# One stage of an eight-stage kernel rewritten: sparse attention with its loop unrolled and its work spread over three engines

## The chip, the core and the metric

The kernel runs on one core of a Trainium2 chip. Its engines are TensorE (PE; PEld is its weight load), VectorE (DVE), ScalarE (ACT), GpSimd (POOL) and SyncE (SP, which issues DMAs). They run at the same time and wait for one another on semaphores. PE writes to PSUM (eight banks, ps in the names), which DVE and ACT read and POOL does not. The metric is the time of one execution in microseconds (us); 0.2% of it is 8 us.

## The reference

Eight stages work one after another on X, 2048 tokens by 128 channels: delta, ternary, chunks, ternary, sparse, local, global, local. The change is in the fifth, sparse attention, x = x + attn(layernorm(x)), with one batch of 2048 tokens and H = 16 heads of DK = 8 channels. Cut to what is computed:

```python
Q, K, V = (proj(Wq, bq), proj(Wk, bk), proj(Wv, bv))
l2 = jnp.linalg.norm(Q, axis=-1)
prob = jnp.exp(jax.nn.log_softmax(Q, axis=-1))
entropy = -jnp.sum(prob * jnp.log(prob + 1e-09), axis=-1)
var = jnp.var(Q, axis=-1, ddof=1)
q_scores = 0.5 * l2 + 0.3 * entropy + 0.2 * var
factor = jnp.clip(jnp.round(q_std / (q_mean + 1e-06) * 10), 3, 10)
_, top_idx = jax.lax.top_k(q_scores, 10)
scores = jnp.einsum('bhud,bhld->bhul', Q_sparse, K) / np.sqrt(DK)
out = jnp.einsum('bhud,bhld->bhud', softmax(scores), V)
return scatter(out at top_idx, rank < factor) @ Wo.T + bo
```

q_std and q_mean are of q_scores over the tokens; Q_sparse is Q at the ten chosen tokens of each head; the second einsum weighs V.

## The kernel before

All stages are built one after another by build_program from the list ORDER; each is a function that opens blocks. In a block each engine has its own straight list of instructions, kept in the order written; no scheduler moves them. Between blocks all engines meet, and clear_signals (L45) zeroes the semaphores. X stays in SBUF as 16 tiles of 128 tokens.

sparse_attention (L1742) has three parts. A short block transposes the four weight matrices (L1793, L1799) and POOL fills the row of token numbers tokrow (L1785). A hardware loop of four passes (L1803) follows, each over a group of four tiles. In a pass DVE copies the group (L1838) and normalises it (normalize_tiles, L1169, with inv_sqrt, L84: ten small ops). PE transposes it, ACT evicts it to xnT (L1827), PE makes q and v (L1814, L1815) and k (L1818), DVE adds the biases (L1843, L1844) and makes the three scores of each head from q: the norm of q by its squares and one more inv_sqrt, the variance, and the entropy, for which ACT does Exp (L1831) and Ln (L1833). PE transposes the scores (L1821), DVE keeps them in qs (L1877). Only one buffer and one bank of each kind exist, and link makes DVE wait for its own last instruction.

The third part is the selection block, from L1902 on. DVE finds the ten largest scores of each head by two rounds of eight (L1974 to L1978), then mean and variance of the scores (L1981 to L1984) and u, the number of ranks kept (L1985 to L1995). With the indices spread over all partitions (L1997, L1910, L2000) it builds sel, a one-hot of 16 tiles by 160 columns (L2002), by which PE gathers the chosen queries (L1921). The 160 queries are handled as two halves of 80 (g = 0, 1): scores against all keys (L1929), row maximum (L2017), Exp on ACT (L1964), scaling (L2022), transposes (L1936) and three copies (L2025). Both halves use banks 0 to 3 for scores and 4 to 6 for transposes, so half 1 waits for half 0. Then the contexts in one sum of 160 columns (L1941), the output matrix (L1946), and the scatter by the one-hot selT (L2010) into four banks (L1954), which DVE adds to X (L2033) after the bias (L2031).

## Time and profile before

| | |
|---|---|
| median of 3 runs | 3910.77 us (3905.14 to 3911.5) |
| profiled execution | 3910.19 us |
| its span, first to last instruction | 3908.4 us |
| mean granted clock of TensorE | 0.943 |
| busy in the span | PE 3422.6 (88%), DVE 2563.9 (66%), ACT 1828.0 (47%), POOL 1582.6 (40%) |
| sparse stage | from about 1300 to 1501 us of the span |

The profiled execution's time stands 1.8 us above its span, which leaves out what lies before the first and after the last instruction. A busy share is an average over all eight stages; for the change, the rows of the stage alone count.

### The profile page before, as it was taken

How to read it: one execution, taken by the hardware profiler on the slowest of the kernel's cores; microseconds unless marked ns; L12 is line 12 of the kernel's file. 1: busy time of each engine (PE TensorE's matmuls, PEld its weight loads, DVE VectorE, ACT ScalarE, POOL GpSimd, SP SyncE). 2: the span in 40 equal slices, each digit the busy share in tenths (PEclk: the TensorE clock that was granted, in tenths of full speed). 3: DMA queues.
4: the chain of work that ended last, by engine and by line, in shares of the span. 5: the costliest groups of instructions: out<-in, count | busy, mean ns of one | idle time of the engine just before them, and what ended most of it. 6: DMA issues, size and time to landing. Idle time of an engine off the chain costs nothing. (4 is left out here: it accounts for less than half of the span.)

```text
span 3908.4 us, 61702 instructions
## 1 busy us (share of the span) xinstructions
PE 3422.6 (88%) x23454; PEld 2133.2 (55%) x23454; DVE 2563.9 (66%) x4849; ACT 1828.0 (47%) x3254; POOL 1582.6 (40%) x1085
## 2 busy tenths in 40 slices
...
GB/s 93 1 1 1 1 1 1 1 1 1 1 51 3 5 0 44 2 2 2 38 1 1 1 1 1 1 1 1 1 1 1 1 1 1 1 44 2 2 2 12
DMA packets 21485, 31.44 MB, mean 8 GB/s; under 512 B 8418, under 2 KB 17932, under 8 KB 19724
## 3 DMA queue, kind: packets, MB, share of 16 engines
...
## 5 line engine op out<-in xcount | busy, mean ns | idle before, releaser
L2924 POOL TENSOR_TENSOR global_acc_pool<-global_acc_pool,global_probs 128x1024 f32<-128x1024 f32 x320 | 776.2, 2426 | 470.7 <-ACT global_probs L2877 453.9
L2877 ACT ACTIVATE global_probs<-global_ps 128x1024 f32<-128x1024 f32 x512 | 524.4, 1024 | 883.3 <-PE global_ps L2750 822.2
L2972 DVE TENSOR_REDUCE global_part<-global_ps 128x2 f32<-128x1024 f32 x512 | 624.5, 1220 | 429.7 <-PE global_ps L2732 429.6
L2750 PE MATMUL global_ps<-global_q,global_k 64*128 64x512 f32 x2048 | 522.4, 588 | 0.0
L2761 PE MATMUL global_ps<-global_probs,global_v 128*64 128x512 f32 x2048 | 495.7, 605 | 0.0
L2732 PE MATMUL global_ps<-global_khh,global_qhh 64*128 64x512 f32 x1024 | 324.9, 631 | 35.7 <-DVE global_part L2972 33.6
L994 DVE COPY_PREDICATED delta_Y<-delta_tri,delta_ps 128x512 f32<-128x512 uint32 x192 | 140.3, 731 | 290.9 <-PE delta_ps L533 290.9
L2748 PE MATMUL global_ps<-global_mrow,global_first 64*128 64x512 f32 x1024 | 323.6, 629 | 0.0
L900 POOL TENSOR_TENSOR delta_gm<-C_tile,delta_g 128x1024 f32<-128x1024 f32 x16 | 30.3, 1896 | 719.2 <-PE delta_ps L453 685.5
L2761 PEld LDWEIGHTS global_ps<-global_probs,global_v 128*64 128x64 f32 x2048 | 124.2, 136 | 282.6 <-issue 161.5
L2732 PEld LDWEIGHTS global_ps<-global_khh,global_qhh 64*128 64x128 f32 x1024 | 97.9, 188 | 322.7 <-DVE global_part L2972 259.1
L811 ACT ACTIVATE delta_T<-delta_ps 128x512 f32<-128x512 f32 x192 | 114.7, 597 | 270.2 <-PE delta_ps L496 270.2
L2750 PEld LDWEIGHTS global_ps<-global_q,global_k 64*128 64x128 f32 x2048 | 193.9, 186 | 86.0 <-issue 61.3
L375 PE MATMUL delta_ps<-delta_wconv,delta_x1T 128*128 128x512 f32 x512 | 232.7, 599 | 6.3 <-PEq L50 5.1
L2301 ACT ACTIVATE local_sm<-local_ps,local_nb,local_rn 128x128 f32<-128x128 f32 x512 | 226.3, 463 | 15.9 <-DVE local_nb L2487 14.5
L2924 DVE TENSOR_TENSOR global_acc<-global_acc,global_probs 128x1024 f32<-128x1024 f32 x128 | 194.8, 1522 | 10.1 <-ACT global_probs L2877 10.1
L518 PE MATMUL delta_ps<-delta_T,delta_NT 128*128 128x128 f32 x1536 | 195.1, 278 | 0.7 <-ACT delta_T L811 0.7
L533 PE MATMUL delta_ps<-delta_Y,delta_NTp 128*128 128x128 f32 x1536 | 192.8, 279 | 0.0
L2748 PEld LDWEIGHTS global_ps<-global_mrow,global_first 64*128 64x128 f32 x1024 | 96.4, 185 | 163.4 <-issue 151.9
L518 PEld LDWEIGHTS delta_ps<-delta_T,delta_NT 128*128 128x128 f32 x1536 | 183.1, 191 | 4.2 <-ACT delta_T L811 0.9
L533 PEld LDWEIGHTS delta_ps<-delta_Y,delta_NTp 128*128 128x128 f32 x1536 | 181.4, 191 | 0.0
L375 PEld LDWEIGHTS delta_ps<-delta_wconv,delta_x1T 128*128 128x128 f32 x512 | 94.5, 192 | 102.8 <-issue 100.7
...
## 6 DMA issues: line engine op xcount, KB each, us to landing
delta_cw<-in_conv_taps SPq DMA_DIRECT2D x4, 1024.0 KB, 10.5
...
global_cos<-in_rope_cos SPq DMA_DIRECT2D x2, 512.0 KB, 10.5
...
```

The lines of the kernel that those rows point to most:

```text
L375: mm = pe.matmul(banks(bank), x1T[:, P * n + j:P * n + j + P], wconv[:, j, column:column + 512], start=(j == 0), stop=(j == TAPS - 1))
L518: mm = pe.matmul(bank_heads(NTP_BANK[s], 1)[:, h % 4, :], NT[:, h, :], T[:, h, :], start=True, stop=True)
L533: mm = pe.matmul(bank_heads(DELTA_BANK[s], 1)[:, h % 4, :], NTp[:, h, :], Y[:, n % 2, h, :], start=True, stop=True)
L994: dve.copy_predicated(Y[:, n % 2, half(s), :], over_middle(tri[:, l + 1, :], 4), bank_heads(DELTA_BANK[s], 1)).then_inc(PAIRED["Y_ready"][ ...
L2301: ins = act.activation(sm[:, k % 2, g, :], ps[:, SC + part, P * i:P * i + P], ACT.Exp, bias=nb[:, k % 2, g:g + 1], scale=rn[:, k % RN, hea ...
L2732: mm = pe.matmul(ps[:, 5 + s, :], qhh[own, u % 2, P * qt:P * qt + P], khh[own, group_of(u) % 2, BLK * c:BLK * c + BLK], start=True, stop=True)
L2748: pe.matmul(ps[:, 2 * (at % 2) + s, :], first[own, :], mrow[own, u % 2, :], start=True, stop=False)
L2750: mm = pe.matmul(ps[:, 2 * (at % 2) + s, :], k2[own, group_of(u) % 2, P * k:P * k + P], q[own, u % 3, :], start=False, stop=True)
L2761: mm = pe.matmul(ps[own, 4, :], v[:, k, HD * g:HD * g + HD], probs[:, at % RING, BLK * s:BLK * s + BLK], start=(k == 0), stop=(k == TILES ...
L2877: act.activation(probs[:, at % RING, :], ps[:, 2 * (at % 2):2 * (at % 2) + 2, :].rearrange("p b n -> p (b n)"), ACT.Exp).then_inc(S["probs ...
L2924: ins = eng.tensor_tensor(sums[:, u % 2, :], sums[:, u % 2, :], probs[:, at % RING, :], ALU.add)
L2972: dve.tensor_reduce(part[:, u % 2, r % SLOTS, :], ps[:, 5:7, :], X_AXIS, ALU.max)\
```

## The change

The loop and the short block before it become one block over all 16 tiles. The normalisation is done once for 16 tiles, with inverse_root (nine ops), as the ternary stage does it. Each kind of PSUM result has two banks in turn. The biases of q and v become matmuls with one row (ones by the bias) into the same bank. ACT evicts q, its square, v and k. POOL adds the output bias to X, subtracts the mean, squares the difference, and multiplies probabilities by their logarithms. One inverse_root over 256 columns serves the norms of all groups. In the selection block ACT makes sum and squared spread of the scores, sel is made in quarters, POOL makes selT, each half has four banks of its own, the contexts are two sums of 80 columns, and X is added by group. The rank numbers are loaded in the first block.

```diff
--- before
+++ after
+GROUPS = TILES // GROUP
+TURN_BANKS, Q_BANKS, V_BANKS, K_BANKS = (0, 1), (2, 3), (4, 5), (6, 7)
+GATHER_BANK, IDX_BANK, COLS_BANK = 4, 5, 6
...
-with nc.Fori(0, TILES // GROUP) as t:
...
+        pool.memset(tiny[:], 1e-9).then_inc(S["constants"], 1)
+        pool.iota(tokrow[:], [[1, TOKENS]], base=0, channel_multiplier=0,
+                  allow_small_or_imprecise_dtypes=True)
+        pool.wait_ge(E["arena_loaded"], C["arena_count"])
+        pool.wait_ge(S["xn_ready"], GROUPS)
+        pool.tensor_tensor(X[:], X[:], over_middle(bo, TILES), ALU.add).then_inc(S["bias_added"], 1)
+        for g in range(GROUPS):
+            pool.wait_ge(S["mean_ready"], g + 1)
+            q8 = q_all[:, GROUP * g:GROUP * g + GROUP, :].rearrange("p t (h e) -> p (t h) e", e=HD)
+            pool.tensor_tensor(dev[:, g], q8, over_inner(s1[:, g], HD), ALU.subtract)\
+                .then_inc(S["centred"], 1)
+            pool.wait_ge(S["centred"], 2 * g + 1)
+            pool.tensor_tensor(dev[:, g], dev[:, g], dev[:, g], ALU.mult).then_inc(S["centred"], 1)
+        for g in range(GROUPS):
+            pool.wait_ge(S["log_ready"], g + 1)
+            pool.tensor_tensor(lp[:, g], lp[:, g], e8[:, g], ALU.mult).then_inc(S["weighed"], 1)
...
+        def project(g, banks, i, bias):
+            for t in range(GROUP):
+                own = ps[:, banks[g % 2], P * t:P * t + P]
+                pe.matmul(own, xnT[:, g % 2, P * t:P * t + P], wT[:, i, :], start=True, stop=False)
+                mm = pe.matmul(own, ones[0:1, :], bias[0:1, :], start=False, stop=True)
+            return mm
+        def project_all(g):
+            pe.wait_ge(S["xnT_ready"], g + 1)
+            if g >= 2:
+                pe.wait_ge(S["q_ready"], g - 1)
+            project(g, Q_BANKS, 0, bq).then_inc(S["q_ps"], 1)
+            if g >= 2:
+                pe.wait_ge(S["v_ready"], g - 1)
+            project(g, V_BANKS, 2, bv).then_inc(S["v_ps"], 1)
+            if g >= 2:
+                pe.wait_ge(S["k_ready"], g - 1)
+            pe.matmul(ps[:, K_BANKS[g % 2], :], wT[:, 1, :], xnT[:, g % 2, :], start=True, stop=True)\
+                .then_inc(S["k_ps"], 1)
...
+        for g in range(GROUPS):
+            turn_rows(g)
+            if g == 0:
+                pe.wait_ge(S["wT_ready"], 1)
+            project_all(g)
...
+        def keep_rows(g):
+            act.wait_ge(S["xnT_ps"], g + 1)
+            if g >= 2:
+                act.wait_ge(S["k_ps"], g - 1)
+            act.activation(xnT[:, g % 2, :], ps[:, TURN_BANKS[g % 2], :], ACT.Copy).then_inc(S["xnT_ready"], 1)
+        def keep_projections(g):
+            tiles = slice(GROUP * g, GROUP * g + GROUP)
+            act.wait_ge(S["q_ps"], g + 1)
+            act.activation(q_all[:, tiles, :].rearrange("p t d -> p (t d)"), ps[:, Q_BANKS[g % 2], :], ACT.Copy)
+            act.activation(sq[:, g].rearrange("p h e -> p (h e)"), ps[:, Q_BANKS[g % 2], :], ACT.Square)\
+                .then_inc(S["q_ready"], 1)
+            act.wait_ge(S["v_ps"], g + 1)
+            act.activation(v_all[:, tiles, :].rearrange("p t d -> p (t d)"), ps[:, V_BANKS[g % 2], :], ACT.Copy)\
+                .then_inc(S["v_ready"], 1)
+            act.wait_ge(S["k_ps"], g + 1)
+            act.activation(kT_all[:, GT * g:GT * g + GT], ps[:, K_BANKS[g % 2], :], ACT.Identity, bias=bk)\
+                .then_inc(S["k_ready"], 1)
+        for g in range(GROUPS):
+            keep_rows(g)
+            keep_projections(g)
+        for g in range(GROUPS):
+            act.wait_ge(S["shifted"], g + 1)
+            act.activation(e8[:, g], e8[:, g], ACT.Exp).then_inc(S["exp_ready"], 1)
+        act.wait_ge(S["constants"], 1)
+        for g in range(GROUPS):
+            act.wait_ge(S["prob_ready"], g + 1)
+            act.activation(lp[:, g], e8[:, g], ACT.Ln, bias=tiny[:]).then_inc(S["log_ready"], 1)
+        for g in range(GROUPS):
+            act.wait_ge(S["scoreT_ps"], g + 1)
+            act.activation(qs[:, GT * g:GT * g + GT], ps[0:H, g, :], ACT.Copy).then_inc(S["scoreT_ready"], 1)
...
+        def sums(g):
+            dve.wait_ge(S["q_ready"], g + 1)
+            q8 = q_all[:, GROUP * g:GROUP * g + GROUP, :].rearrange("p t (h e) -> p (t h) e", e=HD)
+            link(dve.tensor_reduce(s1[:, g], q8, X_AXIS, ALU.add))
+            dve.tensor_scalar(s1[:, g], s1[:, g], 1.0 / HD, None, ALU.mult).then_inc(S["mean_ready"], 1)
+            link(dve.tensor_reduce(m8[:, g], q8, X_AXIS, ALU.max))
+            dve.tensor_tensor(e8[:, g], q8, over_inner(m8[:, g], HD), ALU.subtract).then_inc(S["shifted"], 1)
+            dve.tensor_reduce(s2[:, g], sq[:, g], X_AXIS, ALU.add)
+        def probs(g):
+            dve.wait_ge(S["exp_ready"], g + 1)
+            link(dve.tensor_reduce(den8[:, g], e8[:, g], X_AXIS, ALU.add))
+            link(dve.reciprocal(den8[:, g], den8[:, g]))
+            dve.tensor_tensor(e8[:, g], e8[:, g], over_inner(den8[:, g], HD), ALU.mult)\
+                .then_inc(S["prob_ready"], 1)
+        def variances(g):
+            dve.wait_ge(S["centred"], 2 * g + 2)
+            return dve.tensor_reduce(var8[:, g], dev[:, g], X_AXIS, ALU.add)
+        def entropies(g):
+            dve.wait_ge(S["weighed"], g + 1)
+            return dve.tensor_reduce(ent[:, g], lp[:, g], X_AXIS, ALU.add)
+        for g in range(GROUPS):
+            sums(g)
+            if g:
+                probs(g - 1)
+        probs(GROUPS - 1)
+        every = {n: a[:].rearrange("p g h -> p (g h)") for n, a in
+                 (("s2", s2), ("l2", l2), ("var8", var8), ("ent", ent))}
+        link(dve.tensor_scalar(every["s2"], every["s2"], SMALLEST, None, ALU.max))
+        link(inverse_root(dve, link, every["s2"], every["l2"], t1[:], t2[:]))
+        link(dve.tensor_tensor(every["l2"], every["l2"], every["s2"], ALU.mult))
+        for g in range(GROUPS):
+            ins = variances(g)
+        link(ins)
+        link(dve.tensor_scalar(every["var8"], every["var8"], 0.2 / (HD - 1), None, ALU.mult))
+        link(dve.scalar_tensor_tensor(out=every["l2"], in0=every["l2"], scalar=0.5, in1=every["var8"],
                                       op0=ALU.mult, op1=ALU.add))
...
+        for g in range(GROUPS):
+            ins = entropies(g)
+        link(ins)
+        dve.scalar_tensor_tensor(out=score[:].rearrange("p t h -> p (t h)"), in0=every["ent"], scalar=-0.3,
+                                 in1=every["l2"], op0=ALU.mult, op1=ALU.add).then_inc(S["score_ready"], 1)
...
+    for part in range(4):
+        pe.wait_ge(A["sel_ready"], part + 1)
+        for t in range(4 * part, 4 * part + 4):
+            mm = pe.matmul(ps[:, GATHER_BANK, 0:H * TOP], q_all[:, t, :], sel[:, t, :],
+                           start=(t == 0), stop=(t == TILES - 1))
+    mm.then_inc(A["gather_ps"], 1)
+    pe.wait_ge(A["u_ready"], 1)
...
+    def turn_probs(g):
         pe.wait_ge(A["probs_ready"], g + 1)
...
+        for t in range(TILES):
+            mm = pe.transpose(ps[:, 4 * g + t // 6, HALF * (t % 6):HALF * (t % 6) + HALF],
+                              probs[:, g, P * t:P * t + P], ident[0:HALF, 0:HALF])
         mm.then_inc(A["probsT_ps"], 1)
...
+    def contexts(g):
+        pe.wait_ge(A["probsT_ready"], g + 1)
+        for t in range(TILES):
+            mm = pe.matmul(ps[:, 4 * g + 3, 0:HALF], v_all[:, t, :], probsT[:, g, t, :],
+                           start=(t == 0), stop=(t == TILES - 1))
+        mm.then_inc(A["o_ps"], 1)
+    def rows_out(g):
+        pe.wait_ge(A["oT_ready"], g + 1)
+        pe.matmul(ps[0:HALF, 5 + g, 0:DIM], oT[:, 8 * g:8 * g + 8, :].rearrange("p h r -> p (h r)"),
+                  wT[:, 3, :], start=True, stop=True).then_inc(A["ow_ps"], 1)
+    turn_probs(0)
+    contexts(0)
+    turn_probs(1)
+    contexts(1)
+    rows_out(0)
+    rows_out(1)
...
+    act.activation(spare[:], qs[:], ACT.Copy, accum_out=total[:]).then_inc(A["total_ready"], 1)
+    act.wait_ge(A["total_ready"], 1)
+    act.activation(nst[:], total[:], ACT.Copy, scale=-1.0 / TOKENS).then_inc(A["nmean_ready"], 1)
+    act.wait_ge(A["nmean_ready"], 1)
+    act.activation(spare[:], qs[:], ACT.Square, bias=nst[:], accum_out=ur[:]).then_inc(A["spread_ready"], 1)
...
+@block.gpsimd
+def _(pool):
+    for g in range(2):
+        pool.wait_ge(A["cols_ready"], 1)
+        pool.tensor_scalar(selT[:, g, :], tokrow[:], idxcol[:, g:g + 1], None, ALU.is_equal)\
+            .then_inc(A["selT_ready"], 1)
...
+    dve.tensor_tensor(zexp[:], over_middle(topf[:, 0:TOP], H), over_inner(ident[0:H, 0:H], TOP), ALU.mult)\
+        .then_inc(A["z_ready"], 1)
+    dve.wait_ge(A["idx_ps"], 1)
+    dve.tensor_copy(idx[:], ps[:, IDX_BANK, 0:H * TOP]).then_inc(A["idx_ready"], 1)
+    dve.wait_ge(A["idx_ready"], 1)
+    for part in range(4):
+        own = slice(4 * part, 4 * part + 4)
+        dve.tensor_tensor(sel[:, own], over_middle(idx[:], 4), over_inner(tokid[:, own], H * TOP), ALU.is_equal)\
+            .then_inc(A["sel_ready"], 1)
...
+    def scale_probs(g):
         dve.wait_ge(A["probs_exp"], g + 1)
...
+        own = srow[:, g:g + 1]
+        link(dve.reciprocal(own, own))
+        link(dve.tensor_tensor(own, own, valid[:], ALU.mult))
+        dve.tensor_scalar(probs[:, g, :], probs[:, g, :], own, None, ALU.mult).then_inc(A["probs_ready"], 1)
+    def keep_probs(g):
         dve.wait_ge(A["probsT_ps"], g + 1)
         for b, n in enumerate((6, 6, 4)):
...
+            ins = dve.tensor_copy(probsT[:, g, 6 * b:6 * b + n, :],
+                                  ps[:, 4 * g + b, 0:HALF * n].rearrange("p (i r) -> p i r", r=HALF))
         ins.then_inc(A["probsT_ready"], 1)
...
+    scale_probs(0)
+    scale_probs(1)
+    keep_probs(0)
+    keep_probs(1)
+    own_heads(0)
+    own_heads(1)
+    dve.wait_ge(S["bias_added"], 1)
+    for g in range(GROUPS):
+        dve.wait_ge(A["y_ps"], g + 1)
+        own = X[:, GROUP * g:GROUP * g + GROUP, :].rearrange("p t d -> p (t d)")
+        dve.tensor_tensor(own, ps[:, g, :], own, ALU.add)
```

**ACT, groups.** Before, one pass of the loop (run four times):

```order
L1827 ACT_TABLE_LOAD
L1827 ACTIVATE sparse_xnT<-sparse_ps 128x512
L1829 ISA
L1829 ACTIVATE sparse_kT_all<-sparse_ps,inputs_arena 128x512
L1831 ACTIVATE sparse_e<-sparse_e 128x512
L1833 ACT_TABLE_LOAD
L1833 ACTIVATE sparse_lp<-sparse_e,sparse_tiny 128x512
```

Now, from the last group's evictions (the first of five rows, like those of the three groups before) to the end of the block:

```order
L1867 ACTIVATE sparse_xnT<-sparse_ps 128x512
L1872 ACTIVATE sparse_q_all<-sparse_ps 128x512
L1873 ACTIVATE sparse_sq<-sparse_ps 128x512
L1876 ACTIVATE sparse_v_all<-sparse_ps 128x512
L1879 ACTIVATE sparse_kT_all<-sparse_ps,inputs_arena 128x512
L1887 ACTIVATE sparse_e<-sparse_e 128x512 x4
L1891 ACT_TABLE_LOAD
L1891 ACTIVATE sparse_lp<-sparse_e,sparse_tiny 128x512 x4
L1894 ACTIVATE sparse_qs<-sparse_ps 16x512 x4
```

All four Exps (sparse_e) stand behind the evictions of all four groups.

**PE, selection block.** Before:

```order
L1910 MATMUL sparse_ps<-sparse_zexp,C_tile 128x160
L1914 MATMUL sparse_ps<-C_tile,sparse_idx 80x1 x2
L1916 MATMUL sparse_ps<-sparse_u,C_tile 80x1
L1921 MATMUL sparse_ps<-sparse_sel,sparse_q_all 128x160 x16
L1929 MATMUL sparse_ps<-sparse_kT_all,sparse_qexp 80x512 x4
L1936 MATMUL sparse_ps<-C_tile,sparse_probs 128x80 x16
L1929 MATMUL sparse_ps<-sparse_kT_all,sparse_qexp 80x512 x4
L1936 MATMUL sparse_ps<-C_tile,sparse_probs 128x80 x16
L1941 MATMUL sparse_ps<-sparse_probsT,sparse_v_all 128x160 x16
```

Now, from the same place:

```order
L1983 MATMUL sparse_ps<-sparse_zexp,C_tile 128x160
L1988 MATMUL sparse_ps<-sparse_sel,sparse_q_all 128x160 x16
L1993 MATMUL sparse_ps<-C_tile,sparse_idx 80x1 x2
L1995 MATMUL sparse_ps<-sparse_u,C_tile 80x1
L2001 MATMUL sparse_ps<-sparse_kT_all,sparse_qexp 80x512 x8
L2008 MATMUL sparse_ps<-C_tile,sparse_probs 128x80 x16
L2015 MATMUL sparse_ps<-sparse_probsT,sparse_v_all 128x80 x16
L2008 MATMUL sparse_ps<-C_tile,sparse_probs 128x80 x16
L2015 MATMUL sparse_ps<-sparse_probsT,sparse_v_all 128x80 x16
```

The scores of both halves run together, the column matmuls stand behind the gather, and each half has its own context sum.

## Rows read from the trace of the kernel before

**Rows 1.** Windows of the stage: busy us of each engine (records), granted clock, DMA.
```profile
1300.21:1304.39 4.18, 0.63 (x4) 0.42 (x4) 0.01 (x2) 0.78 (x2) 1.87 (x2) 0.78 0.02 6
1304.39:1422.91 118.52, 28.84 (x104) 19.78 (x104) 76.24 (x228) 20.69 (x25) 0.00 (x0) 0.56 0.00 0
1422.91:1500.88 77.97, 35.49 (x188) 28.14 (x188) 43.30 (x62) 5.70 (x6) 0.00 (x0) 0.70 0.00 0
```
**Rows 2.** Timeline, start of the second pass: start, us, line, output<-input [idle before].
```profile
1334.25 0.43 DVE L1838 COPY sparse_xg<-X 128x512 f32 x1 [1.59 <-PEq L50]
```
**Rows 3.** Timeline of the ternary stage just before.
```profile
1283.33 3.19 DVE L1271 BATCH_NORM_STATS2 ternary_gstats<-X 128x6 f32<-128x128 f32 x16 [1.93 <-PEq L50]
...
1289.85 7.08 DVE L1287 TENSOR_SCALAR ternary_xn<-X,ternary_gmv,ternary_grstd 128x128 f32<-128x128 f32 x16
...
1291.11 1.26 POOL L1261 TENSOR_TENSOR X<-X,inputs_tern_bias 128x512 f32<-128x512 f32 x1 [36.48 <-DVE ternary_xn L1287]
```
**Rows 4.** Timeline of the first pass, xn to projections.
```profile
1308.37 1.11 DVE L1180 TENSOR_SCALAR sparse_xn<-sparse_xg,sparse_gmv,sparse_grstd 128x128 f32<-128x128 f32 x4
...
1311.34 0.79 PE L1814 MATMUL sparse_ps<-sparse_wT,sparse_xnT 128*128 128x128 f32 x2 [0.69 <-ACT sparse_xnT L1827]
...
1314.91 1.68 PE L1818 MATMUL sparse_ps<-sparse_xnT,sparse_wT 128*128 128x512 f32 x2
```
**Rows 5.** Windows, columns as in rows 1: clock before and after its changes.
```profile
1306.00:1316.00 10.00, 5.78 (x22) 4.63 (x22) 3.77 (x20) 0.60 (x1) 0.00 (x0) 0.50 0.00 0
1316.00:1319.00 3.00, 0.59 (x1) 0.00 (x0) 2.93 (x6) 1.32 (x2) 0.00 (x0) 0.96 0.00 0
...
1459.60:1463.00 3.40, 0.00 (x0) 0.00 (x0) 2.44 (x2) 0.88 (x1) 0.00 (x0) 1.00 0.00 0
1463.00:1466.00 3.00, 0.07 (x1) 0.07 (x2) 1.59 (x3) 1.18 (x2) 0.00 (x0) 0.50 0.00 0
```
**Rows 6.** Groups by line, DVE in the loop: busy us, mean ns, idle before.
```profile
L1859 DVE TENSOR_TENSOR sparse_t<-sparse_qg,sparse_s 128x512 f32<-128x512 f32 x4 | 2.8, 693 | 0.1
...
L1852 DVE TENSOR_REDUCE sparse_s<-sparse_t 128x64 f32<-128x512 f32 x4 | 2.7, 686 | 0.1
...
L1864 DVE RECIPROCAL sparse_s<-sparse_s 128x64 f32<-128x64 f32 x4 | 2.2, 553 | 0.1
...
L95 DVE SCALAR_TENSOR_TENSOR sparse_r<-sparse_r,sparse_s 128x64 f32<-128x64 f32 x4 | 0.9, 226 | 0.1
```
**Rows 7.** Groups by line, ACT in the loop.
```profile
L1827 ACT ACT_TABLE_LOAD x4 | 5.1, 1283 | 18.2 <-PEq L50 18.2
...
L1829 ACT ACTIVATE sparse_kT_all<-sparse_ps,inputs_arena 128x512 f32 x4 | 2.7, 687 | 21.0 <-PE sparse_ps L1818 21.0
...
L1827 ACT ACTIVATE sparse_xnT<-sparse_ps 128x512 f32<-128x512 f32 x4 | 2.4, 597 | 20.7 <-PE sparse_ps L1810 20.7
```
**Rows 8.** Timeline of the selection part.
```profile
1434.89 2.27 DVE L1981 TENSOR_REDUCE sparse_st<-sparse_qs 16x1 f32<-16x2048 f32 x1
...
1444.58 0.31 DVE L1997 TENSOR_TENSOR sparse_zexp<-sparse_topf,C_tile 16x160 f32<-16x160 f32 x1
...
1446.24 2.83 DVE L2002 TENSOR_TENSOR sparse_sel<-sparse_idx,inputs_arena 128x2560 f32<-128x2560 f32 x1
...
1449.12 6.38 PE L1921 MATMUL sparse_ps<-sparse_sel,sparse_q_all 128*128 128x160 f32 x32 [1.91 <-DVE sparse_sel L2002]
...
1472.61 2.29 DVE L2017 TENSOR_REDUCE sparse_mrow<-sparse_ps 80x1 f32<-80x2048 f32 x1 [2.62 <-PE sparse_ps L1929]
...
1475.12 1.96 ACT L1964 ACTIVATE sparse_probs<-sparse_ps,sparse_mrow 80x2048 f32<-80x2048 f32 x1 [10.94 <-DVE sparse_mrow L2018]
...
1478.92 2.39 PE L1936 MATMUL sparse_ps<-C_tile,sparse_probs 80*128 80x80 f32 x16 [6.35 <-DVE sparse_probs L2022]
...
1483.03 6.49 PE L1941 MATMUL sparse_ps<-sparse_probsT,sparse_v_all 128*128 128x160 f32 x32 [1.71 <-DVE sparse_probsT L2025]
...
1491.07 7.41 PE L1954 MATMUL sparse_ps<-sparse_ow,sparse_selT 80*128 80x128 f32 x64 [0.47 <-ACT sparse_ow L1967]
```

More of the change, by code:

```diff
@@ new lines, in _ @@
+                    link(ins)
+                    link(dve.tensor_scalar(B["var"][:], B["mv"][:, :, 1], LN_EPS, None, ALU.add))
+                    link(inverse_root(dve, link, B["var"][:], B["rstd"][:], B["tmp"][:, 0, :], B["tmp"][:, 1, :]))
+                    for t in range(TILES):
+                        ins = dve.tensor_scalar(xn[:, t, :], X[:, t, :], B["mv"][:, t, 0:1], B["rstd"][:, t:t + 1],
+                                                ALU.subtract, ALU.mult)
+                        if t % GROUP == GROUP - 1:
+                            ins.then_inc(S["xn_ready"], 1)
@@ L1917, in _ @@
                     .then_inc(A["cols_ps"], 1)
-                pe.wait_ge(A["sel_ready"], 1)
-                for i in range(TILES):
-                    mm = pe.matmul(ps[:, 7, 0:H * TOP], q_all[:, i, :], sel[:, i, :],
-                                   start=(i == 0), stop=(i == TILES - 1))
-                mm.then_inc(A["q_ps"], 1)
                 pe.wait_ge(A["qexp_ready"], 1)
+                pe.wait_ge(A["cols_ready"], 1)
                 for g in range(2):
-                    if g:
-                        pe.wait_ge(A["probs_exp"], 1)
@@ L1953, in _ @@
+                turn_probs(0)
[4 more added lines that the diff above has]
+                rows_out(1)
+                pe.wait_ge(A["ow_ready"], 2)
+                pe.wait_ge(A["selT_ready"], 2)
+                for t in range(TILES):
                     for g in range(2):
-                        mm = pe.matmul(ps[:, i // 4, P * (i % 4):P * (i % 4) + DIM], selT[:, g, P * i:P * i + P],
-                                       ow[:, g, :], start=(g == 0), stop=(g == 1))
@@ new lines, in _ @@
+                for g in range(2):
+                    act.wait_ge(A["ow_ps"], g + 1)
+                    act.activation(ow[:, g, :], ps[0:HALF, 5 + g, 0:DIM], ACT.Copy).then_inc(A["ow_ready"], 1)
+            @block.gpsimd
+            def _(pool):
+                for g in range(2):
+                    pool.wait_ge(A["cols_ready"], 1)
+                    pool.tensor_scalar(selT[:, g, :], tokrow[:], idxcol[:, g:g + 1], None, ALU.is_equal)\
+                        .then_inc(A["selT_ready"], 1)
```

265 lines of the change are left out of this document (87 added, 178 removed).

## The prediction

> **What bounds the kernel now.** First the windows of the stage [rows 1]. The sparse stage stands alone: VectorE (DVE) leaves the ternary stage at 1300.21, four loop passes run from 1304.39 to 1422.91, the selection part ends at 1500.88. Nothing of another stage overlaps it, so what it saves comes off the span one for one. In the 118.5 us of loop DVE is busy 76.2, TensorE (PE) 28.8, ScalarE (ACT) 20.7, GpSimd (POOL) 0: one chain runs DVE, PE, ACT, DVE in turn, 29.6 us a pass. Then the timeline: 1.6 us between passes go to clearing semaphores and the branch [rows 2]. The selection part is the same kind of chain, 78.0 us with DVE busy 43.3.
>
> **The change, first part.** The loop becomes one block. I follow its longest chain.
>
> 1. DVE starts about 1.2 us after 1300.21 (a block change costs 1.6 with a branch [rows 2]): 1301.4. Statistics and root chain for 16 tiles took 6.5 us in the ternary stage (1283.33 to 1289.85 [rows 3]), now once and not four times a shorter one: 1307.9. Four tiles of xn, four transposes and one eviction: from 1308.37 to 1311.34 before, 3.0 [rows 4]. Projections start at 1310.9.
> 2. Projections. q and v bias move from DVE to 1-row matmuls, so PE has 32 records a group where it had 16. A record took 0.22 us before (16 from 1311.34 to 1314.91 [rows 4]); the clock was at 0.50 of full speed, 1.2 GHz, and rose to 2.4 GHz 4.8 us after the projections began, too late for them [rows 4, 5]. Now there is work left then: 4.8 us hold 21.5 records, the other 10.5 go at the fast rate of 0.116 (64 records in 7.41 [rows 8]), 1.2 us, and k at 0.86 (half of its 1.7): group 0 ends at 1317.8. The next group can't start at once: ACT evicts k (0.69) before it evicts the next transposes (0.60) [rows 7]. A cycle is 32 x 0.116 + 0.86 + 0.69 + 0.60 + 0.2 of handing over = 6.1 us with PE idle 1.4 of it; between 1459.60 and 1463.00 an idle PE still had 1.00 [rows 5], so I take the clock as kept. Three cycles: 1336.1.
> 3. All Exps stand on ACT behind all evictions, as the order shows. So DVE does the sums of groups 0 and 1, then waits about 12 us for the first Exp: k's eviction and Exp, 0.7 each, give 1337.5. This is what is late next.
> 4. DVE then has, of what the loop did, two groups of sums (three reduces, one subtract at 0.69, one small op at 0.2, gaps: 3.1 each) and four of normalising (reduce 0.69, reciprocal 0.55, product 0.69, gaps: 2.05) [rows 6]: 14.4 us, 1351.9. The variance's subtract and square and the product with the logarithm are POOL's now, q's square ACT's, the copies of X and q are gone.
> 5. One root chain on 128x256, not four on 128x64. No such row exists; between 0.226 (64 wide) and 0.693 (512 wide) [rows 6] lies 0.43 for the eight two-input ops, and I take 0.3 for the three others: 4.6 with gaps. The bounds are 2.5 (all as 64 wide) and 7.9 (all as 512 wide). Then eight reduces of 0.69 and three small ops: 6.9. 1363.4.
> 6. POOL at work beside DVE. While POOL added the bias in the ternary stage, 16 tiles of xn took 7.08 us against 1.11 for four alone (4.4 for 16), a factor 1.6 [rows 3, 4]. On the path some 8 us of DVE's work fall beside POOL's: from nothing, if its products don't mind, to 5 us at that factor; no row decides, I take the middle, 2.5. 1365.9. POOL's X add, and its work on groups 0 and 1, lie beside DVE's wait and cost nothing; without that wait (an earlier Exp) they would meet the DVE sums.
> 7. Sixteen score transposes at 0.22 and ACT's last copy, 4.4; block change 1.2: the selection part starts at 1371.5 instead of 1422.91. **51 us saved.**
>
> The Trainium skill, in SBUF — State Buffer, section Who interferes with whom, holds that a DVE instruction in a two-port mode or with two SBUF inputs shares a port with POOL and that one of them blocks; in GPSIMD Engine Reference, section When to use GPSIMD, it advises elementwise work on DVE. By that rule step 6 would be a rival rather than 2.5 us; it is the second below.
>
> **The change, second part**, in us after its start. The count's mean and variance leave DVE's path: 1434.89 to 1444.58, 9.7 us, now two ACT passes beside the top-k search, the short rest behind sel. sel comes in quarters: PE starts three quarters of 2.83 earlier, 2.1. So the gather starts at 26.2 - 9.7 - 2.1 = 14.4 and, at 6.4 as before, ends at 20.8 [rows 8]. The u chain (18 ops of 1 column, about 0.18) ends at 19.9 under it. Column matmuls, copies and the valid mask follow: scores start at 22.0. Each half is four matmuls of 512 columns, 0.86 each at the fast rate as k above: half 0 is ready 3.7 later. Maximum and Exp from 25.7: 2.5 and 2.1, to 30.3 (before, 1472.61, 1475.12 and the Exp's end with its sum [rows 8]). Half 1's scores now use other banks, 29.2; its maximum ends at 31.7, Exp at 33.9. DVE scales half 0 only after that maximum, 1.7: 33.4; transposes 2.4, 35.9; copies 1.7, 37.6 (1478.92 to 1483.03 for the two [rows 8]). The contexts are two sums of 32 records of 80 columns. No such record exists; 0.20 at the low clock (160 columns: 6.49 for 32 in all), 0.12 at the high as above: bounds 3.7 and 6.5, I take 5.4 for the first, since PE is cold from its wait [rows 5], 4.5 for the second. First: 43.0. Transposes of half 1, hot, 1.3; copies 1.6: 46.0; second context 50.5. oT, output product, copy 1.1; scattering 7.4, then the last quarter's add 0.8 [rows 8]: 59.8 against 78.0. selT runs on POOL from 22.0: by POOL's 1.3 us for 512 elements of a sum [rows 3] at most 10 us for both, done well before 51. **18 us saved.** The cleared semaphores and the rank load lie beside other work. The bias to X, 2.3 us, was hidden before.
>
> **Sum.** 51.4 + 18.2 = 69.6. The profiled execution took 3910.2, of which the span is 3908.4 and 1.8 lies around it; the median of the runs is 3910.8, so it stands for them. 3910.2 - 69.6 gives 3841.
>
> **Rivals.**
> - **PE stays at 1.2 GHz in the projections** (0.14). For it: every cycle has an idle stretch, and the loop's projections never left 0.50 before their end [rows 4, 5]. Against it: the clock outlived an idle stretch of 3.4 us. A cycle becomes 32 x 0.223 + 1.7 + 1.5 = 10.3, three times 4.2 more, and 2 in group 0: 3856. TensorE: Matmul & The Clock Gate, section A second HAM failure mode, of the Trainium skill tells of just this, a matmul stream throttled again by short idles between bank changes.
> - **POOL and DVE take turns** (0.12). POOL's products for groups 2 and 3 and the four with the logarithm come while DVE is on the path: eight of 1.3 us [rows 3], 10.4, and selT against the scaling of half 0, 3. In place of 2.5 that gives 3852.
> - **Less in the way than taken** (0.12). No contention (2.5), contexts at 3.7 each (2.5), the root chain at its lower bound (2): 3834.
> - **Slower** (0.03). Four passes of one loop body become straight code. If an engine had to wait for its code, each wait on the path as long as ACT's 4.6 at the head of a pass (18.2 for four [rows 7]), the gain of 69.6 would be gone from the sixteenth wait on; twenty make 92 us, 3933. Against it: the selection part is straight code already, and its 64 scatter records ran with no gap [rows 8].
> - That the change doesn't do what it says: three engines get work but in part take turns, DVE waits 12 us for ACT. That is in the forecast.
>
> **How the numbers follow.** The forecast holds 0.59, its own range 3833 to 3849 from steps 5, 6 and the contexts. The range for 8 in 10 takes in the clock and the port cases with a few us: 3831 to 3859. A difference of 0.2%, 8 us, is what measurement can tell; all cases but the last are faster by more: 0.96 faster, 0.01 same, 0.03 slower.
>
> **What would show it.** Right: DVE idle for about 12 us before the first reduce over e8, ended by ACT's Exp; a projection cycle near 6 us at granted clock 1.00 from the second group on; root ops on 256 columns near 0.43; selection part near 60 us. Wrong: cycles of 10 us at 0.50; DVE products of 512 near 1.1 or more beside POOL; DVE idle before the variance or entropy reduces, ended by POOL; a longer local stage; gaps that nothing explains in the unrolled block.

## The result, and the profile after

The changed kernel takes 3881.82 us (median of 4 runs, 3877.67 to 3885.77) against 3911.14 of the kernel before (3905.14 to 3911.82): ratio 0.9928, 95% interval 0.9915 to 0.9941. It is faster, by 29 us and not by 70: outside the range of 3831 to 3859. The profiled execution took 3877.67, its span is 3875.9, 32.5 shorter than before.

Windows of the stage (columns as in rows 1: width, busy us of PE, PEld, DVE, ACT and POOL, granted clock, DMA's share and GB/s): statistics, five stretches of the projections, the two context sums, the scatter:

```profile
1299.00:1307.00 8.00, 0.63 (x4) 0.42 (x4) 6.72 (x46) 0.60 (x1) 1.89 (x2) 0.66 0.01 0
1309.60:1324.00 14.40, 14.39 (x38) 9.26 (x38) 4.19 (x10) 2.37 (x4) 6.94 (x3) 0.50 0.01 2
1324.70:1339.00 14.30, 14.30 (x38) 9.35 (x38) 3.14 (x5) 2.32 (x4) 2.44 (x2) 0.50 0.00 0
...
1339.80:1342.30 2.50, 2.43 (x12) 1.77 (x12) 0.00 (x0) 0.01 (x1) 0.00 (x0) 1.00 0.00 0
...
1353.10:1356.00 2.90, 2.90 (x15) 2.05 (x15) 0.00 (x0) 0.00 (x0) 0.00 (x0) 1.00 0.00 0
...
1356.50:1364.40 7.90, 7.90 (x19) 4.50 (x18) 0.00 (x0) 1.68 (x3) 0.00 (x0) 0.50 0.00 0
...
1437.40:1444.40 7.00, 7.00 (x34) 7.00 (x34) 0.00 (x0) 0.00 (x0) 0.00 (x0) 0.50 0.00 0
...
1448.30:1455.20 6.90, 6.88 (x32) 6.88 (x33) 0.11 (x1) 0.00 (x0) 0.00 (x0) 0.50 0.00 0
1456.80:1471.00 14.20, 14.03 (x64) 13.73 (x64) 2.17 (x4) 0.00 (x0) 0.00 (x0) 0.50 0.00 1
```

PE is busy without a break within each group of the projections; between groups it waits 0.69 us for ACT to evict the transposes. The clock is at 0.50, its lower level of 1.2 GHz, but for the two short stretches at 1.00 at the head of the third and fourth groups, and it falls back to 0.50 there with PE busy. In the loop before, PE was busy 28.8 of 118.5 us [rows 1]; now it bounds the first part. Timeline of PE and of its weight loads (PEld) at the start of the projections, where rows 4 stood before:

```profile
1309.52 0.77 PE L1825 MATMUL sparse_ps<-sparse_wT,sparse_xnT 128*128 128x128 f32 x2 [0.78 <-ACT sparse_xnT L1867]
1310.22 0.79 PE L1826 MATMUL sparse_ps<-inputs_arena,C_tile 1*128 1x128 f32 x2
1310.94 0.80 PE L1825 MATMUL sparse_ps<-sparse_wT,sparse_xnT 128*128 128x128 f32 x2
1311.66 0.79 PE L1826 MATMUL sparse_ps<-inputs_arena,C_tile 1*128 1x128 f32 x2
```
```profile
1310.21 0.50 PEld L1826 LDWEIGHTS sparse_ps<-inputs_arena,C_tile 1*128 1x128 f32 x2 [0.22 <-issue]
1310.94 0.50 PEld L1825 LDWEIGHTS sparse_ps<-sparse_wT,sparse_xnT 128*128 128x128 f32 x2 [0.23 <-issue]
1311.66 0.50 PEld L1826 LDWEIGHTS sparse_ps<-inputs_arena,C_tile 1*128 1x128 f32 x2 [0.23 <-issue]
```

A matmul (two records) starts each 0.72 us, a q or v row in L1825 and its bias in L1826 by turns. Ahead of each pair of loads stand 0.22 us of idle with nothing to wait for. I had taken 0.22 a record, 0.44 a matmul. What that does to DVE, and DVE's work after it, in its timeline:

```profile
1334.23 0.67 DVE L1920 TENSOR_REDUCE sparse_s<-sparse_sq 128x64 f32<-128x512 f32 x1
1365.68 0.69 DVE L1924 TENSOR_REDUCE sparse_den<-sparse_e 128x64 f32<-128x512 f32 x1 [30.78 <-ACT sparse_e L1887]
1366.40 0.55 DVE L1925 RECIPROCAL sparse_den<-sparse_den 128x64 f32<-128x64 f32 x1
1366.99 0.69 DVE L1926 TENSOR_TENSOR sparse_e<-sparse_e,sparse_den 128x512 f32<-128x512 f32 x1
...
1369.13 1.07 DVE L1919 TENSOR_TENSOR sparse_e<-sparse_q_all,sparse_m 128x512 f32<-128x512 f32 x1
...
1379.75 1.35 DVE L1944 TENSOR_SCALAR sparse_s<-sparse_s 128x256 f32<-128x256 f32 x1
1381.13 1.23 DVE L3167 TENSOR_SCALAR sparse_l<-sparse_s 128x256 int32<-128x256 int32 x1
1382.40 1.36 DVE L3168 TENSOR_TENSOR sparse_t<-sparse_l 128x256 f32<-128x256 f32 x1
1383.80 0.43 DVE L3169 TENSOR_TENSOR sparse_t<-sparse_t,sparse_s 128x256 f32<-128x256 f32 x1
```

The wait for the first Exp is 30.78 us where I had 12. Three operations of the root chain (1.35, 1.23, 1.36) lie beside the products with the logarithm that POOL ran from 1378.01 to 1383.49; the next, with POOL idle, takes 0.43. The selection part's timeline, from the first half's transposes, where before stood the last rows of rows 8:

```profile
1433.25 2.40 PE L2008 MATMUL sparse_ps<-C_tile,sparse_probs 80*128 80x80 f32 x16 [4.91 <-DVE sparse_probs L2113]
...
1437.36 7.12 PE L2015 MATMUL sparse_ps<-sparse_probsT,sparse_v_all 128*128 128x80 f32 x32 [1.71 <-DVE sparse_probsT L2118]
...
1444.27 2.34 PE L2008 MATMUL sparse_ps<-C_tile,sparse_probs 80*128 80x80 f32 x16
...
1448.32 7.12 PE L2015 MATMUL sparse_ps<-sparse_probsT,sparse_v_all 128*128 128x80 f32 x32 [1.71 <-DVE sparse_probsT L2118]
...
1456.84 14.03 PE L2034 MATMUL sparse_ps<-sparse_ow,sparse_selT 80*128 80x128 f32 x64 [0.36 <-ACT sparse_ow L2053]
...
1473.14 2.03 DVE L2668 BATCH_NORM_STATS2 local_gstats<-X 128x6 f32<-128x128 f32 x10 [1.54 <-PEq L50]
```

The scatter takes 14.03 us for the same 64 records that took 7.41 [rows 8]. From the last ternary operation to the last X add the stage takes 172.5 us (1299.07 to 1471.59) where it took 200.7 (1300.21 to 1500.88) and where I had 131.1 (1300.2 to 1431.3). The miss of 41 us divides into 29.3 until the first Exp is done (66.6 for 37.3), -0.6 from there to the selection part (33.4 for 34.0), and 12.7 in that part (72.5 for 59.8). Of the 32.5 us of span, 28.9 are there when the local stage begins (1473.14 for 1501.99).

### The profile page after: what moved, and what is told of

The parts are those of the page before. It is cut to its first block and busy times, and to the rows that moved or that the text cites. A ratio compares the mean times of both kernels' runs of the same rounds, so it can differ in the third digit from the quotient of the medians.

```text
span 3875.9 us, 61610 instructions
## 1 busy us (share of the span) xinstructions
PE 3460.4 (89%) x23550; PEld 2161.1 (56%) x23550; DVE 2522.3 (65%) x4730; ACT 1832.9 (47%) x3269; POOL 1613.7 (42%) x1100
## 6 DMA issues: line engine op xcount, KB each, us to landing
delta_cw<-in_conv_taps SPq DMA_DIRECT2D x4, 1024.0 KB, 11.5
```

## The experiments

**Theory A**: PE pulls no weight load under a running matmul when matmuls of different row counts take turns (q and v rows 128, bias 1), and the projections with 1-row matmuls and the sums of 80 columns a load stay at 1.2 GHz. **Rivals**: the accumulation onto one region stalls the load (B); it is the number of matmuls alone (C); gaps of PE keep the clock down; ACT's order is what costs.

Length of the projections below runs from their first matmul to the end of the last k eviction; of the stage, from its first DVE operation to the end of the last X add. Both are from the timeline of each run's one profile. The 196.5 of the kernel before starts with the loop's first pass, 4.2 us behind the last ternary operation; that of the others with the first sparse block. Time is the median.

| kernel | time, us | projections | stage |
|---|---|---|---|
| before | 3911.1 | in the loop | 196.5 |
| changed | 3881.8 | 55.6 | 171.7 |
| e1_wide_bias | 3854.0 | 26.0 | 141.4 |
| e2_bank_bias | 3867.6 | 40.1 | 155.5 |
| e3_no_bias | 3847.3 | 18.8 | 134.3 |
| e13_64_rows | 3884.1 | 57.7 | 174.5 |
| e7_exp_order | 3880.7 | 60.4 | 166.5 |
| e12_wide_exp | 3843.9 | 27.1 | 133.7 |
| e4_dve_bias | 3848.9 | 23.3 | 130.9 |
| e5_one_context | 3870.1 | 55.4 | 156.3 |
| e6_contexts_last | 3878.7 | 59.9 | 171.5 |
| e9_dve_one | 3826.8 | 23.3 | 115.7 |
| e14_sel_dve | 3823.8 | 23.3 | 114.0 |
| e15_lp_dve | 3829.2 | 23.3 | 114.6 |

**1. The bias as a 128-row matmul.**

```
-  mm = pe.matmul(own, ones[0:1, :], bias[0:1, :], start=False, stop=True)
+  mm = pe.matmul(own, ident, bias, start=False, stop=True)
```

> Bias as a 128-row matmul (the identity as weights, the bias rows streamed) in place of the 1-row one; as many matmuls, and the same accumulation. Theory A (a 1-row matmul beside a 128-row one keeps the next weight load from being pulled under the running matmul, and 1-row matmuls keep the granted clock down): no idle of 0.22 us ahead of the loads, a matmul each 0.44 us at half clock and 0.23 at full, the clock rises in the first group, the projections fall from 54.9 to 28 to 32 us, time 3853 to 3862. Rival B (the accumulation onto the same region stalls the load): still 0.72 us a matmul, 3880. Rival C (only the number of matmuls counts, the clock stays at 0.50): 0.44 us a matmul, cycle 10.8 us, projections 43 us, time 3868.

3854.02 us (ratio to before 0.9849, 0.983 to 0.9868). Timelines of PE and of the loads:

```profile
1316.33 0.64 PE L1826 MATMUL sparse_ps<-inputs_arena,C_tile 128*128 128x128 f32 x2
1316.76 0.63 PE L1825 MATMUL sparse_ps<-sparse_wT,sparse_xnT 128*128 128x128 f32 x2
1317.18 0.63 PE L1826 MATMUL sparse_ps<-inputs_arena,C_tile 128*128 128x128 f32 x2
```
```profile
1316.12 0.55 PEld L1826 LDWEIGHTS sparse_ps<-inputs_arena,C_tile 128*128 128x128 f32 x2
1316.55 0.55 PEld L1825 LDWEIGHTS sparse_ps<-sparse_wT,sparse_xnT 128*128 128x128 f32 x2
```

Its windows of PE alone (width, busy with records, granted clock, DMA):

```profile
1315.70:1322.00 6.30, 6.23 (x32) 0.55 0.01 4
1322.00:1328.00 6.00, 5.17 (x41) 1.00 0.00 0
1328.00:1341.20 13.20, 11.34 (x80) 1.00 0.01 2
```

As many matmuls and the same accumulation, yet one each 0.43 us at half clock, no idle ahead of a load, and 1.00 from the end of the first group on. B and C are out. From the last ternary operation to the selection part it takes 70.3 us, and I had forecast 71.3 for the first part.

**2. No bias on q and v.**

```
-  pe.matmul(own, xnT[...], wT[:, i, :], start=True, stop=False)
-  mm = pe.matmul(own, ones[0:1, :], bias[0:1, :], start=False, stop=True)
+  mm = pe.matmul(own, xnT[...], wT[:, i, :], start=True, stop=True)
```

> No bias on q and v (it is left out of the result). Theory A and rivals B and C alike: 0.44 us a matmul at half clock, 0.23 at full; cycle 4 to 5 us after the clock has risen, projections 20 to 24 us, and DVE's wait for the first Exp falls from 30.8 to under 4 us; time 3846 to 3852. This is the ceiling of what the bias matmuls cost. If the time stays above 3870 the projections are not what the forecast missed.

3847.28 us (0.9837, 0.982 to 0.9853), as expected. So the 1-row matmuls cost 34.5 us together, and in their 128-row form 6.7. Two terms missed all the same: the projections take 18.8 us, less than the 20 expected, and DVE's wait for the first Exp is 7.0 us, not under 4.

**3. One 1-row matmul a bank.**

```
+  pe.matmul(ps[:, banks[g % 2], :], ones[0:1, :], over_middle(bias[0:1, :], GROUP), start=True, stop=False)
   for t in range(GROUP):
-      pe.matmul(own, xnT[...], wT[:, i, :], start=True, stop=False)
-      mm = pe.matmul(own, ones[0:1, :], bias[0:1, :], start=False, stop=True)
+      mm = pe.matmul(own, xnT[...], wT[:, i, :], start=False, stop=(t == GROUP - 1))
```

> One 1-row matmul of 512 columns per bank puts the bias of four tiles in, then four 128-row matmuls accumulate. Theory A: the row change happens twice a bank instead of eight times, so 0.3 us of stall a bank; by the k matmul's 2.08 us at half clock for 512 columns a bank is 2.1 + 1.8 + 0.3 = 4.2 us, a group 12 us at half clock and 7 at full; projections 35 to 46 us, time 3861 to 3872. Rival B (accumulation stalls): the four mains keep 0.72 us each, 5.0 us a bank, projections 50 us, time 3877.

3867.56 us (0.9884, 0.9867 to 0.99). The start of its projections:

```profile
1321.75 2.07 PE L1823 MATMUL sparse_ps<-inputs_arena,C_tile 1*128 1x512 f32 x2
1323.75 2.08 PE L1825 MATMUL sparse_ps<-sparse_wT,sparse_xnT 128*128 128x128 f32 x8
```

A bank takes 2.00 us of bias and 2.0 of its four sums, 4.0 and not B's 5.0; time and projections (40.1 us) are in Theory A's ranges. The projections' clock is 0.65 for a while (1330 to 1344) and 0.50 at the end (1344 to 1357).

**4. 64 rows in place of one.**

```
-  mm = pe.matmul(own, ones[0:1, :], bias[0:1, :], start=False, stop=True)
+  mm = pe.matmul(own, ident[0:64, :], bias[0:64, :], start=False, stop=True)
```

> The changed kernel with a 64-row matmul (identity as weights, bias rows streamed) in place of the 1-row one: it adds the bias to half of the tokens alone, so that the result is not the reference's. It asks what of a 1-row matmul does the harm. If any change in the number of rows keeps the load from being pulled ahead: 0.72 us a matmul at half clock, as with one row; but the clock may rise as more rows are active: projections 36 to 55 us, 3862 to 3882. If it is few rows alone: 0.43 us a matmul, projections 26 us, 3853 to 3858.

3884.08 us (0.9916, 0.9896 to 0.9935), the changed kernel's time. Its PE and load timelines:

```profile
1319.03 0.79 PE L1826 MATMUL sparse_ps<-inputs_arena,C_tile 64*128 64x128 f32 x2
1319.75 0.79 PE L1825 MATMUL sparse_ps<-sparse_wT,sparse_xnT 128*128 128x128 f32 x2
```
```profile
1319.02 0.50 PEld L1826 LDWEIGHTS sparse_ps<-inputs_arena,C_tile 64*128 64x128 f32 x2 [0.22 <-issue]
1319.75 0.50 PEld L1825 LDWEIGHTS sparse_ps<-sparse_wT,sparse_xnT 128*128 128x128 f32 x2 [0.23 <-issue]
```

The same 0.72 us and the same 0.22 of idle. It is the change of the row count that does it, not that one row is few; the scatter, 80 rows in every matmul, has no such idle. The clock stays down here too (0.50 over the 11.70 us from 1318.30, PE busy 11.67; 0.54 over the next 46, in which the third group began with matmuls 0.42 us apart for 3 us). The Trainium skill (TensorE: Matmul & The Clock Gate, section The mechanism of Part 3) has a load pulled ahead of a running matmul where its row group doesn't conflict or where it goes to the background weight buffer, and further down says that loads overlap running matmuls only where the row groups differ. That last sentence doesn't agree with these rows: with equal rows the loads run under the matmuls without idle (experiment 1), with 64 against 128, or 1 against 128, 0.22 us of idle stand ahead of each pair.

**5. ACT's order.** The Exp of group g-1 behind the evictions of group g:

```
   for g in range(GROUPS):
       keep_rows(g)
       keep_projections(g)
+      if g:
+          exponential(g - 1)
-  for g in range(GROUPS):
-      act.wait_ge(S["shifted"], g + 1)
-      act.activation(e8[:, g], e8[:, g], ACT.Exp).then_inc(S["exp_ready"], 1)
+  exponential(GROUPS - 1)
```

> ACT takes the Exp of group g-1 right after the evictions of group g, instead of all four behind all evictions; nothing else changes. Theory: three of the four normalising steps (2.05 us each on DVE) and three Exps fall into DVE's wait, so score is ready 5 to 7 us earlier: 3875 to 3877. Rival (ACT pays a table load of 1.3 us at each switch between Exp and Copy, six switches, and the evictions that PE waits for come later): 0 to 8 us lost, 3882 to 3890.

3880.71 us (0.9914, 0.9898 to 0.9931; the changed kernel had 0.9928): no difference that can be told. No table load was paid at the switches between Exp and Copy. The stage is 5.2 us shorter in the profile: the order gained 10 us behind the projections, but these are 4.8 us longer (60.4 for 55.6), since the changed kernel's two stretches at 1.00 are missing: 0.50 from 1316.1 to 1376. That the order took them away is not shown. The second kernel of experiment 7 has the changed kernel's projections line for line, and they took 59.9 us. Its window of PE over them:

```profile
1310.10:1369.30 59.20, 57.10 (x148) 0.50 0.00 1
```

So the same projections took 55.4, 55.6 and 59.9 us in three profiles, by whether the clock rose in them. What the rows show of the order itself is 0.5 us: PE waits 0.93 in place of 0.69 for ACT's eviction ahead of the last two groups. The 5.2 us of the stage do not show in the times; what lies behind the stage took 2411.0 us in this profile, 2404.3 in the changed kernel's.

> The bias as 128-row matmuls and ACT's Exp of group g-1 behind the evictions of group g. Theory: with PE's cycle near 6 us instead of 15, DVE's waiting is short, so normalising on the way saves at most the wait for the first Exp that the 128-row kernel still has; the evictions PE waits for come 0.6 us later each. Expected 3 to 7 us less than the 128-row kernel's 3854. Rival (as with the 1-row biases, where this order gave 1 us): no difference, or the clock is not raised and it is over 5 us slower.

The same order with the 128-row bias: 3843.93 us (0.9829, 0.9813 to 0.9846), 10 less than experiment 1 by the medians, more than the 3 to 7 expected, though single runs of the two overlap; the stage is 7.7 shorter (141.4 to 133.7). DVE waited 11.5 us for the Exp in experiment 1 and does not wait for it here.

**6. The biases on DVE** as it evicts, with ACT's order of 5. PE's bias matmuls go, and ACT squares q from the evicted copy; of the edit, the evictions alone:

```
-  act.activation(q_all[...], ps[:, Q_BANKS[g % 2], :], ACT.Copy)
-  act.activation(v_all[...], ps[:, V_BANKS[g % 2], :], ACT.Copy)
+  dve.tensor_tensor(q_all[:, own, :], ps[:, Q_BANKS[g % 2], :]..., over_middle(bq, GROUP), ALU.add)
+  dve.tensor_tensor(v_all[:, own, :], ps[:, V_BANKS[g % 2], :]..., over_middle(bv, GROUP), ALU.add)
```

> q and v biases added by DVE as it evicts the banks (two tensor_tensor of 128x512 a group), no bias matmuls; ACT squares q from SBUF and takes the Exp of group g-1 behind the evictions of group g. Theory: projections as without a bias, 19 to 23 us; DVE gains 8 additions of 0.7 us, of which most lie in its waits for PE: the stage is 136 to 142 us long against 171.7 of the changed kernel, time 3847 to 3854. Rival (DVE is now what bounds each group: 0.7 + 3.1 + 0.7 + 2.1 = 6.6 us a group behind a PE cycle of 4.5): the stage 143 to 148 us, 3855 to 3860.

3848.92 us (0.9834, 0.9817 to 0.985), with the shortest stage so far, 130.9, 2.9 under experiment 5's second kernel. The times say the opposite (3848.9 for 3843.9); what lies behind the stage took 2414.0 us in this profile and 2404.3 in the other, though it is the same code. The rival's mechanism is there: DVE waits for PE 1.0 us in all, so it sets the cycle, 6.35 us a group for the rival's 6.6, and the projections take 23.3 us where without a bias they take 18.8. The stage is 5 us under the theory's lower end all the same, and 12 under the rival's; the expectation does not say of what its stage is added up, so which term was too high stays open.

**7. The contexts.** One sum of 160 columns for both halves, behind the transposes of both (the layout of probsT and the waits follow; not shown):

```
-  mm = pe.matmul(ps[:, 4 * g + 3, 0:HALF], v_all[:, t, :], probsT[:, g, t, :], ...)
+  mm = pe.matmul(ps[:, 3, 0:H * TOP], v_all[:, t, :], probsT[:, t, :], ...)
```

> The changed kernel, but both halves' probabilities go into one 160-column context sum after both transposes, as in the kernel before; banks and everything else as changed. Theory A (matmuls of 80 columns a weight load keep the granted clock at 0.50; those of 160 raise it, as before, and the scatter behind them runs at 1.00): contexts 6.5 to 7.1 us once in place of twice, scatter 7.4 us in place of 14.0; the stage 12 to 14 us shorter, time 3868 to 3871. Rival (the scatter is slow for another reason, its waits or POOL): scatter stays at 14.0, only one context sum is saved: 3875.

3870.06 us (0.989, 0.9873 to 0.9906). Its timeline:

```profile
1445.15 7.36 PE L2015 MATMUL sparse_ps<-sparse_probsT,sparse_v_all 128*128 128x160 f32 x32 [1.71 <-DVE sparse_probsT L2117]
...
1453.88 7.41 PE L2033 MATMUL sparse_ps<-sparse_ow,sparse_selT 80*128 80x128 f32 x64 [0.36 <-ACT sparse_ow L2052]
```

and the windows of its PE:

```profile
1443.50:1450.00 6.50, 4.84 (x18) 0.50 0.00 0
1450.00:1452.00 2.00, 2.00 (x14) 0.80 0.00 0
1452.00:1456.00 4.00, 3.30 (x27) 1.00 0.00 0
```

The clock rises within the sum, and the scatter finds it there: 7.41 us. The stage is 15.3 us shorter.

> The changed kernel with both halves' transposes first and then the two 80-column context sums back to back, with no gap of PE between them. Theory A (it is the 80 columns a load): both stay at 7.1 us, the scatter at 14.0, the granted clock at 0.50; time within 3 us of the changed kernel's 3882. Rival (the gaps and transposes between the two sums kept the clock down): it rises during 14 us of unbroken sums, the second takes 3.6 to 5 us and the scatter 7.4: 3871 to 3875.

```
   turn_probs(0)
+  turn_probs(1)
   contexts(0)
-  turn_probs(1)
   contexts(1)
```

Both transposes first, then two sums of 80 columns back to back: 3878.65 us (0.9919, 0.9902 to 0.9935). The stage is as long as the changed kernel's, but of two parts: the projections 4.3 us longer, as told in experiment 5, and the selection part 4.5 shorter (68.0 for 72.5), as PE no longer waits twice 1.71 us for DVE's copies ahead of the sums. Its windows of PE:

```profile
1438.90:1443.40 4.50, 4.50 (x32) 0.50 0.00 0
1443.50:1450.00 6.50, 6.50 (x32) 0.50 0.00 0
1450.00:1452.00 2.00, 2.00 (x12) 0.50 0.00 0
1452.00:1456.00 4.00, 4.00 (x20) 0.50 0.00 0
```

PE is busy 19.2 of the 19.4 us from 1437.6 to 1457 at 0.50, and the scatter takes 14.02. Gaps are not the reason: behind the same transposes the clock stayed at 0.50 through both sums of 80 columns a load and rose within the sum of 160.

**8. Together.** Experiment 6 with the one context sum of 7:

> The kernel with DVE's biases and the moved Exps (3848.9 us), with the one 160-column context sum beside it. Theory A: the two gains are in different stretches and add: 14 to 15 us less, the stage 115 to 117 us long, scatter 7.4 us: 3833 to 3837. Rival (the clock that the longer sums raised hung on what came before them): contexts and scatter as in the changed kernel, 3841 to 3849.

3826.76 us (0.9783, 0.977 to 0.9797), 6 us under the range expected; the stage, 115.7, is as expected, 15.2 under experiment 6. The gains add.

The selections of rows back to DVE, behind the valid mask:

```
-  pool.tensor_scalar(selT[:, g, :], tokrow[:], idxcol[:, g:g + 1], None, ALU.is_equal)
+  dve.tensor_scalar(selT[:, g, :], tokrow[:], idxcol[:, g:g + 1], None, ALU.is_equal)
```

> The same, with the two selections of rows (80x2048, POOL 5.4 us each) given back to DVE, in its wait for the first scores. Theory: they take 1.3 to 2 us each there, under PE's score matmuls, and the scaling of half 0 falls from 2.05 to 1.28 us as POOL is idle beside it: 0.5 to 1 us less than the kernel without this edit. Rival (POOL beside it costs nothing on the path): same within 0.3 us, or up to 1 us slower if DVE is late for the first scores.

**3823.82 us** (0.9775, 0.9761 to 0.9788; 3821.84 to 3828.99), the fastest by median: 58 us under the changed kernel, 89 under the kernel before as it ran beside it (3913.2). Against e9 the runs overlap. The stage is 1.7 us shorter, but only 0.8 of it is the edit's (the scaling of half 0, 1.28 for 2.05); the context sum took 6.02 us for 7.26, as the clock was at 1.00 some 3 us after its start and not 5. The two selections take 2.48 us together on DVE, 10.88 on POOL.

The products of entropies back to DVE too:

```
-  pool.tensor_tensor(lp[:, g], lp[:, g], e8[:, g], ALU.mult)
+  link(dve.tensor_tensor(lp[:, g], lp[:, g], e8[:, g], ALU.mult))
```

> The same again, with the four products of entropies (128x512, POOL 1.4 us each) done by DVE. Theory (POOL and DVE take turns: what POOL takes from the root chain, 1.35 against 0.29 us for a 128x256 tensor_scalar, about equals what DVE saves): between 1.5 us faster and 1.5 us slower than the kernel without this edit. Rival (POOL's work is a true gain): 2.8 to 4 us slower.

3829.22 us (0.979, 0.9776 to 0.9803; 3825.63 to 3835.22): 5.4 us above e14 by the medians, with runs that overlap; the stages differ by 0.6 us, and the code behind the stage, the same in both, took 5.7 us more in this profile. DVE's timeline in it, beside the rows of the changed kernel above:

```profile
1342.03 0.28 DVE L1950 TENSOR_SCALAR sparse_s<-sparse_s 128x256 f32<-128x256 f32 x1
1342.35 0.29 DVE L3173 TENSOR_SCALAR sparse_l<-sparse_s 128x256 int32<-128x256 int32 x1
1342.68 0.42 DVE L3174 TENSOR_TENSOR sparse_t<-sparse_l 128x256 f32<-128x256 f32 x1
...
1349.96 0.69 DVE L1940 TENSOR_TENSOR sparse_lp<-sparse_lp,sparse_e 128x512 f32<-128x512 f32 x1
```

Without POOL beside them the three take 0.99 us together, not 3.94: 2.95 came from POOL, about the 2.76 that four products cost DVE. So in the stage POOL's help there is worth 0.6 us. The times alone don't rule out the rival's 2.8 to 4 us.

## Why the prediction was wrong, step by step

- **Step 1** was right: 10.45 us from the last ternary operation to the first projection for 10.7.
- **Step 2 failed, and carries 29.3 of the 41 us.** I priced a bias record as a q record (0.22 at 1.2 GHz, 0.116 at 2.4) from rows in which all matmuls had 128 rows, and took the clock to rise after 4.8 us of work as it had there. The row for the new thing, a 1-row matmul between 128-row ones, was not in the trace, and I gave it no bounds. It costs 0.72 us a matmul at half clock, 0.29 more than at equal rows: 64 matmuls, at most 18.6 us. The rest of the 29.6 us between the projections of the changed kernel and of experiment 1, at least 11 us, is the clock. The 29.3 is that of one profile: with no stretch at 1.00, as in experiment 7's second kernel, the same projections are 4.3 us longer. The rival "PE stays at 1.2 GHz" had the clock nearly right (0.56 in mean) and its reason wrong: the first group ran 14.4 us without a break at 0.50, and experiment 1 has idle stretches between its groups too, of 0.83 us, at 1.00. It also lacked the stall, so that its 3856 misses as well. With equal row counts the step as written holds: cycle near 6 us, 1.00 from the second group on.
- **Step 3**: the wait for the first Exp was placed rightly, but sized by step 2 (30.78 for 12). Its cure alone shortened the stage by 5 us and the time by nothing that can be told; once PE was fast it gave 7.7 us of stage and 10 of the median.
- **Steps 4 to 7** were right in sum, 33.4 for 34.0 us, which is partly luck: step 6 was 1.4 too low and the others together 2.0 too high. Step 6, taken at 2.5, measured 3.9: 2.95 in the root chain, 0.18 on the product before it (0.87 for 0.69) and 0.38 on each of the two subtracts of 128x512 on the path (1.07 for 0.69). Its remark on an earlier Exp came true as well: in experiment 6 POOL's add to X (4.53 us) lies beside the first group's sums, and a small tensor_scalar there took 2.33 us for 0.19. The reduces took 0.67 to 0.69 with POOL at work, as without. The Trainium skill (SBUF — State Buffer, section Who interferes with whom) says that a reduce never contends with POOL, while a tensor_scalar can and an operation with two SBUF inputs does; that agrees with these rows.
- **The second part** was right to the start of the contexts (38.3 for 37.6). **What failed is the clock behind them**: contexts 7.12 twice for 5.4 and 4.5, transposes 2.34 for 1.3, and the scatter, taken at 7.4 from rows 8, 14.03. Its 7.4 hung on the 160-column sums that the change had split; I kept the old price of a step whose neighbour had changed. These four terms make 12.0 of 12.7 us.
- **The rivals**: POOL and DVE taking turns was there, at 3.9 us and not 10.4; the selections did delay the scaling, by 0.8 and not 3. Waiting for code was not seen; the 4.6 us a wait that this rival took from rows 7 are idle time of ACT ended by the block change, not by code. "Less in the way" was wrong.
- **Left open**: why the clock stays at 0.50 beside alternating rows. The runs never took the stall and the alternation apart: in the runs where the row count alternates at every matmul both are there, in experiment 1 neither. Experiment 3 comes nearest: its rows change only twice a bank and little stall is left (four sums in 2.0 us, where 0.43 each makes 1.7), yet the clock fell back to 0.50 (1344 to 1357), with the 1-row matmuls taking half of each bank's time. Open too is what decides in one execution whether the clock rises in the changed kernel's projections. Nor is the last of the span's gain, 32.5 - 28.9 = 3.6 us behind the stage, of the change: the same code behind the stage took 2401.6 to 2414.0 us in the fourteen profiles, and the code ahead of it 1299.9 to 1308.8.
